# Three segment-max passes of a graph network: the folded buffer is cut from a batch of nine gathers into nine buffers of three, and the fold takes its state from SBUF instead of PSUM

## The chip, the cores and the metric

The kernel runs on one core of a Trainium2 chip. The metric is the device time of one execution in microseconds, the median of three runs. Lower is better.

## The reference, cut to what matters

There are 6250 nodes with 256 float32 features and 100,000 edges, sorted by destination `dst`. The first layer of the network takes the maximum over each node's incoming edges three times, each time of new features. The second layer is an attention over the same edges.

```python
def _pool_max(h, edge_src, edge_dst):
    pooled = segment_max(h[edge_src], edge_dst, num_segments=N)
    cnt = segment_sum(ones, edge_dst, num_segments=N)
    return where((cnt > 0)[:, None], pooled, 0)

h1 = relu(embeddings @ Wp1.T + bp1)
p1 = _pool_max(h1, edge_src, edge_dst)
x  = relu(concatenate([embeddings, p1], 1) @ Wm1.T + bm1)
p2 = _pool_max(x, edge_src, edge_dst)
y2 = relu(concatenate([x, p2], 1) @ Wm2.T + bm2)
x  = _layernorm(y2 + x, ln2_g, ln2_b)
p3 = _pool_max(x, edge_src, edge_dst)
y3 = relu(concatenate([x, p3], 1) @ Wm3.T + bm3)
x  = _layernorm(y3 + x, ln3_g, ln3_b)
```

## The kernel before, in words

**Layout of a max pass.** The 100,000 edges lie as 783 columns (CH) of 128 edges, one in each of the 128 partitions. A partition holds three chains of 261 consecutive edges (C = 3). Within a chain the running maximum goes from one edge to the next, and is reset where a new destination begins: `new = max(old + reset, gathered)`, where reset is 0 or -1e30. That is one VectorE instruction, the fold (L559, 128 rows of 256 features). A step folds one edge of each chain, three folds that don't depend on each other; each depends on the fold of its chain in the step before. Nine columns (J), which are three steps (STEPS), make a batch, and a pass has 87 batches (NB). Three buffers G[b] (UB) hold a batch of nine gathered rows each.

**What each engine does for a batch.** GpSimd waits for the batch's list of indices (`c_eix`) and for the buffer's last store (`s_hs[b]`), and issues nine indirect gathers of 128 rows of 1 KB from the table in DRAM (L533). VectorE waits once for all nine (`s_eg[b]`), and folds in place. The old state is read from PSUM (`state`, `state2`), where ScalarE has copied it: after folds 0 and 1 of a step one copy of two rows (L597), after fold 2 one of the third row (L599), each after a wait on `c_fold`, each announced on `c_state`, which the next step's folds wait for. After the sixth fold VectorE writes the index list of the batch after the next one (`place`, L540). SyncE waits for the last fold and stores the nine folded rows to a history in DRAM, 1152 KB in one DMA (L581).

**What runs beside it.** The helper `staged` writes the order of each engine's instructions out by hand: a list of stages per batch, one after the other, and each engine works it off in that order with no overtaking. Between VectorE's folds stand other pieces ("fillers"). In all passes they include the layer's own tile: TensorE transposes a tile of 128 nodes (L668), ScalarE evacuates it (L651), TensorE multiplies it with a weight (L674), and VectorE adds the bias and keeps the product (`keep`, L637, which waits for the product); 49 tiles, one in each of the first 50 or so batches. In pass 1 come the one-hots that count edges per node (L952, then TensorE at L1120) and part of a sort; in pass 2 the sort (L810, L825); in pass 3 the spread of its result and a bias (L640). After each pass the history's rows are gathered and combined with U to the next features. After the third pass comes the attention layer (L1453, L1869 and on; L2153 and L2163 are its last tiles).

The functions that the change touches are `max_pass` (L518 to L620), the semaphores (L200 and on) and the one-hots' `vector` (L942 to L965).

## Time and profile before

| quantity | value |
|---|---|
| median of 3 runs | 5532.19 us (5524.11 to 5537.15) |
| span of the profiled execution | 5536.0 us, 24899 instructions |
| GpSimd busy | 3489.2 us (63%) |
| VectorE busy | 3357.0 us (61%) |
| ScalarE busy | 1170.9 us (21%) |
| TensorE matmuls busy | 1120.6 us (20%) |
| pass 1, first to last gather | 82.06 to 1249.65 us |
| pass 2 | 1364.13 to 2461.30 us |
| pass 3 | 2588.30 to 3683.20 us |
| gathers of the passes | 2349 of 951 ns on average |
| DMA queues | software 628.59 MB, 38.1% of the engines' span; hardware 409.34 MB, 19.9% |

An engine's busy share is over the whole span; the three passes, their combine stages and the attention have different limits. Instruction groups are named by line, engine and operation; "out<-in" are the tensors written and read. Some PSUM banks have names like tail, wide and trio, and a row carries the name of the bank or neighbouring allocation, so `tail` and `wide` in the fold's rows stand for `state` and `state2`. "Idle before" is the time in which an engine did nothing ahead of an instruction, by what ended it: "issue" is nothing that the profile shows, "remote" a semaphore whose poster it can't name.

### The profile page before, as it was taken

How to read it: one execution, taken by the hardware profiler on the slowest of the kernel's cores; microseconds unless marked ns; L12 is line 12 of the kernel's file. 1: busy time of each engine (PE TensorE's matmuls, PEld its weight loads, DVE VectorE, ACT ScalarE, POOL GpSimd, SP SyncE). 2: the span in 40 equal slices, each digit the busy share in tenths (PEclk: the TensorE clock that was granted, in tenths of full speed). 3: DMA queues.
4: the chain of work that ended last, by engine and by line, in shares of the span. 5: the costliest groups of instructions: out<-in, count | busy, mean ns of one | idle time of the engine just before them, and what ended most of it. 6: DMA issues, size and time to landing. Idle time of an engine off the chain costs nothing. (4 is left out here: it accounts for less than half of the span.)

```text
span 5536.0 us, 24899 instructions
## 1 busy us (share of the span) xinstructions
PE 1120.6 (20%) x4017; PEld 728.3 (13%) x4017; DVE 3357.0 (61%) x6781; ACT 1170.9 (21%) x2663; POOL 3489.2 (63%) x3686
## 2 busy tenths in 40 slices
PE   5333321105222221006222200019400000000005
PEld 4222211004111110005111100016200000000003
DVE  7676666554434434336355433338479888898896
ACT  4222222222222222224222222225100000000001
POOL 4566666665666666665676666654466666666653
PEclk7555555557555555557555555559755555555557
DMA  5555555554555655556555655554477677776763
GB/s 178 170 170 172 173 169 187 183 188 136 197 184 192 203 183 195 185 189 187 199 190 197 217 179 188 188 171 153 139 224 215 212 216 216 224 220 208 218 186 109
DMA packets 325739, 1039.51 MB, mean 188 GB/s; under 512 B 71351, under 2 KB 124740, under 8 KB 292172
## 3 DMA queue, kind: packets, MB, share of 16 engines
q0 software_dynamic: 209408, 628.59, 38.1%
q1 hardware_dynamic: 116172, 409.34, 19.9%
q14 instruction: 125, 1.02, 0.1%
q8 instruction: 34, 0.56, 0.0%
HBM read 649.96 MB, written 388.11 MB: 188 GB/s over the span
## 5 line engine op out<-in xcount | busy, mean ns | idle before, releaser
L533 POOL DMA_INDIRECT G<-tab,ix x2349 | 2233.6, 951 | 1135.8 <-issue 699.7
L559 DVE SCALAR_TENSOR_TENSOR G<-tail,pass_lists,G 128x256 f32<-128x256 f32 x1566 | 696.4, 477 | 1217.8 <-DMA G<-tab,ix 526.8
L1869 POOL DMA_INDIRECT kv<-kvtab,dst_ix x936 | 889.1, 950 | 428.1 <-issue 283.1
L597 ACT ACTIVATE tail<-G 128x512 f32<-128x512 f32 x783 | 470.6, 601 | 1600.4 <-issue 607.7
L599 ACT ACTIVATE wide<-G 128x256 f32<-128x256 f32 x783 | 300.1, 383 | 949.8 <-DVE G L559 521.4
L674 PE MATMUL tail<-weights,hT 128*128 128x256 f32 x588 | 305.0, 674 | 766.3 <-issue 499.6
L559 DVE SCALAR_TENSOR_TENSOR G<-wide,pass_lists,G 128x256 f32<-128x256 f32 x783 | 372.6, 476 | 111.7 <-issue 84.4
L2058 PE MATMUL trio<-ident,state 128*128 128x128 f32 x6 | 2.0, 430 | 1476.8 <-DVEq L2080 1476.8
L674 PEld LDWEIGHTS tail<-weights,hT 128*128 128x128 f32 x588 | 172.7, 324 | 848.9 <-issue 529.1
L1918 DVE TENSOR_TENSOR kv<-kv,wide 128x3072 f32<-128x3072 f32 x78 | 260.8, 3343 | 29.0 <-DMA kv<-kvtab,dst_ix 28.9
L1934 DVE TENSOR_REDUCE s<-kv 128x96 f32<-128x3072 f32 x78 | 260.8, 3343 | 0.0
L2008 ACT ACTIVATE wide<-weights 128x120 f32<-128x120 f32 x78 | 21.4, 274 | 1090.8 <-remote 388.2
L668 PE MATMUL tail<-ident,h 128*128 128x128 f32 x294 | 95.0, 425 | 710.1 <-issue 296.9
L2058 PEld LDWEIGHTS trio<-ident,state 128*128 128x128 f32 x6 | 1.2, 220 | 1477.7 <-DVEq L2080 1477.7
L1120 PE MATMUL trio<-hot 128*128 128x196 bf16 x783 | 140.9, 367 | 240.6 <-DVE hot L952 149.7
L637 DVE TENSOR_TENSOR U<-tail,weights 128x256 f32<-128x256 f32 x147 | 61.3, 417 | 205.8 <-remote 169.5
L952 DVE TENSOR_TENSOR hot<-wide,key_high 128x2156 bf16<-128x2156 f32 x72 | 170.3, 2366 | 10.3 <-issue 5.8
L1394 PE MATMUL trio<-ident,G 128*128 128x128 f32 x18 | 4.5, 424 | 766.0 <-PEq L522 766.0
L668 PEld LDWEIGHTS tail<-ident,h 128*128 128x128 f32 x294 | 41.7, 199 | 818.6 <-issue 760.2
L1120 PEld LDWEIGHTS trio<-hot 128*128 128x128 bf16 x783 | 113.1, 147 | 263.2 <-DVE hot L952 156.5
L1927 DVE TENSOR_TENSOR trio<-kv,wide 128x1536 f32<-128x1536 f32 x78 | 136.5, 1750 | 0.0
L1960 DVE TENSOR_TENSOR pass_lists<-trio,kv 128x1536 f32<-128x1536 f32 x78 | 136.1, 1745 | 0.0
(361 smaller groups left out, 3602.7 us busy)
## 6 DMA issues: line engine op xcount, KB each, us to landing
hist<-G SPq DMA_DIRECT2D x261, 1152.0 KB
G<-tab,ix POOLq DMA_INDIRECT x2349
ahist<-state SPq DMA_DIRECT2D x78, 408.0 KB
tab<-o SPq DMA_DIRECT2D x147, 128.0 KB
kv<-kvtab,dst_ix POOLq DMA_INDIRECT x936
h<-tab SPq DMA_DIRECT2D x98, 128.0 KB
G<-tab SPq DMA_DIRECT2D x98, 128.0 KB
kvtab<-U SPq DMA_DIRECT2D x49, 256.0 KB
```

Of the source, the lines that this page charges most:

```text
L533: g.indirect_dma_start(G[b][:, k, :], None, tab, bass.IndirectOffsetOnAxis(ix[:, b, k:k + 1], 0)).then_inc(s_eg[b].sem, 16)
L559: ins = v.scalar_tensor_tensor(out=G[b][:, k, :], in0=state2 if c == 2 else state[:, c, :], scalar=reset[:, at:at + 1], in1=G[b][:, k, :], ...
L597: a.activation(state, of[:, 0:2, :], ACT.Copy).then_inc(c_state.sem, 1)
L599: a.activation(state2, of[:, 2, :], ACT.Copy).then_inc(c_state.sem, 1)
L668: t = pe.transpose(self.turned[:, k * P:(k + 1) * P], self.h[:, b, k * P:(k + 1) * P], ident[:, :])
L674: m = pe.matmul(self.product, self.hT[:, k * P:(k + 1) * P], self.w[:, k, :], start=(k == 0), stop=(k == KC - 1))
L952: v.tensor_tensor(to[n % self.RING][:, 0:some, :, :].rearrange("p k l e -> p (k l) e"), self.iota[:, None, 0:width].to_broadcast([P, 2 * s ...
L1120: m = pe.matmul(self.sums, self.low[n % self.RING][:, k, :, :], self.high[n % self.RING][:, k, :, :], start=(n == 0 and k == 0), stop=(n = ...
L1869: g.indirect_dma_start(kvs[n % KB][:, k, :], None, kvtab, bass.IndirectOffsetOnAxis(dst_ix[:, at:at + 1], 0)).then_inc(s_kv[n % KB], 16)
L1918: v.tensor_tensor(keys, keys, query[:, None, :, :].to_broadcast([P, SLOT, R, D]), ALU.mult).then_inc(c_scored, 1)
L1927: keep("weighed", i * UB + b, v.tensor_tensor(to.rearrange("p k (d h) -> p k d h", h=HEADS), vals[:, part, :].rearrange("p k (d h) -> p k ...
L1934: keep("sums", i * UB + b, v.tensor_reduce(scores().rearrange("p e r h -> p (e r) h"), kvs[(i * UB + b) % KB][:, :, 0:D].rearrange("p k (h ...
```

## The change

Each of the nine thirds of the three buffers becomes a buffer of its own, with its own semaphores (`s_in[r]` for arrival, `s_kept[r]` for the store). GpSimd waits before every third gather, for the store of that buffer three batches ago, and not once in a batch. VectorE waits for three gathers at a step's first fold, and not for nine at a batch's first. Each fold reads the old state straight from the step before in SBUF, and waits on `c_fold` for the fold three before it, which is its own engine's; all nine folds of a batch post on `c_fold`, where six did. ScalarE's copies, `c_state`, and the waits on it go, those of the one-hots too. SyncE stores each step by itself: three DMAs of 384 KB in place of one of 1152 KB. The sizes, the number of gathers and the order of the fillers on VectorE stay, and so does the place of the index list.

```diff
--- before.py
+++ after.py
@@ -200,10 +200,12 @@
         s_st = [Count(sem(f"s_st{u}")) for u in range(UN)]
         s_put = [sem(f"s_put{u}") for u in range(UN)]
         s_tile = [Count(sem(f"s_tile{b}")) for b in range(UB)]
-        s_eg = [Count(sem(f"s_eg{b}")) for b in range(UB)]
+        RING = UB * STEPS
+        s_in = [Count(sem(f"s_in{r}")) for r in range(RING)]
+        s_kept = [Count(sem(f"s_kept{r}")) for r in range(RING)]
         s_hs = [Count(sem(f"s_hs{b}")) for b in range(UB)]
         c_eix, c_taken, c_batch, c_w, c_e = (Count(sem(n)) for n in ("c_eix", "c_taken", "c_batch", "c_w", "c_e"))
-        c_fold, c_state = Count(sem("c_fold")), Count(sem("c_state"))
+        c_fold = Count(sem("c_fold"))
         s_held = {"vector": sem("s_held_v"), "pool": sem("s_held_p")}
         s_pe = Count(sem("s_pe"))
         s_dve = Count(sem("s_dve"))
@@ -516,8 +518,9 @@
 
 
         def max_pass(G, side, tiles, marks=None, ahead=None):
-            state = bank[3][:, 0:2 * D].rearrange("p (c f) -> p c f", c=2)
-            state2 = bank[6][:, D:2 * D]
+            def rows_of(step):
+                n, j = divmod(step, STEPS)
+                return G[n % UB][:, j * C:(j + 1) * C, :]
 
             with block() as blk:
                 @blk.gpsimd
@@ -528,9 +531,11 @@
 
                     def gather(i, b):
                         g.wait_ge(c_eix.sem, c_eix.of(i, b, UB))
-                        g.wait_ge(s_hs[b].sem, s_hs[b].base + i * 16)
                         for k in range(J):
-                            g.indirect_dma_start(G[b][:, k, :], None, tab, bass.IndirectOffsetOnAxis(ix[:, b, k:k + 1], 0)).then_inc(s_eg[b].sem, 16)
+                            r = b * STEPS + k // C
+                            if k % C == 0 and i:
+                                g.wait_ge(s_kept[r].sem, s_kept[r].base + i * 16)
+                            g.indirect_dma_start(G[b][:, k, :], None, tab, bass.IndirectOffsetOnAxis(ix[:, b, k:k + 1], 0)).then_inc(s_in[r].sem, 16)
                     staged(g, NB, UB, [(0, gather), (0, side.pool(g))])
 
                 @blk.vector
@@ -545,21 +550,19 @@
                     if marks:
                         marks.vector(v)
                     side.start(v)
-                    v.memset(G[UB - 1][:, J - C:J, :], 0.0).then_inc(c_fold.sem, 2)
+                    v.memset(rows_of(UB * STEPS - 1), 0.0).then_inc(c_fold.sem, C)
 
                     def fold(k):
                         def stage(i, b):
                             n, (j, c) = i * UB + b, divmod(k, C)
                             step = n * STEPS + j
-                            if k == 0:
-                                v.wait_ge(s_eg[b].sem, s_eg[b].base + (i * (16 * J) + 16 * J))
-                            if c != 1:
-                                v.wait_ge(c_state.sem, c_state.base + 2 * step + (2 if c else 1))
+                            if c == 0:
+                                arrived = s_in[b * STEPS + j]
+                                v.wait_ge(arrived.sem, arrived.base + (i + 1) * (16 * C))
+                            v.wait_ge(c_fold.sem, c_fold.base + C * step + c + 1)
                             at = c * (CH // C) + step
-                            ins = v.scalar_tensor_tensor(out=G[b][:, k, :], in0=state2 if c == 2 else state[:, c, :], scalar=reset[:, at:at + 1],
-                                                         in1=G[b][:, k, :], op0=ALU.add, op1=ALU.max)
-                            if c:
-                                ins.then_inc(c_fold.sem, 1)
+                            v.scalar_tensor_tensor(out=G[b][:, k, :], in0=rows_of(step - 1 if step else UB * STEPS - 1)[:, c, :], scalar=reset[:, at:at + 1],
+                                                   in1=G[b][:, k, :], op0=ALU.add, op1=ALU.max).then_inc(c_fold.sem, 1)
                             if k == 2 * C - 1:
                                 place((b + 2) % UB, n + 2)
                         return stage
@@ -577,12 +580,14 @@
                     side.sync(sp)
 
                     def store(i, b):
-                        sp.wait_ge(c_fold.sem, c_fold.base + 2 + 2 * STEPS * (i * UB + b + 1))
-                        sp.dma_start(hist_p[:, bass.ds((i * UB + b) * J, J), :], G[b][:, :, :]).then_inc(s_hs[b].sem, 16)
+                        for j in range(STEPS):
+                            step = (i * UB + b) * STEPS + j
+                            sp.wait_ge(c_fold.sem, c_fold.base + C * (step + 2))
+                            sp.dma_start(hist_p[:, step * C:(step + 1) * C, :], G[b][:, j * C:(j + 1) * C, :]).then_inc(s_kept[b * STEPS + j].sem, 16)
                     staged(sp, NB, UB, tiles.sync(sp) + [(0, store)] + (ahead.sync(sp) if ahead else []))
                     side.last_sync(sp)
-                    for b in range(UB):
-                        sp.wait_ge(s_hs[b].sem, s_hs[b].base + (NB // UB) * 16)
+                    for kept in s_kept:
+                        sp.wait_ge(kept.sem, kept.base + (NB // UB) * 16)
 
                 @blk.tensor
                 def _(pe):
@@ -590,31 +595,13 @@
 
                 @blk.scalar
                 def _(a):
-                    def keep_state(step):
-                        n, j = divmod(step, STEPS)
-                        of = G[n % UB][:, j * C:(j + 1) * C, :]
-                        a.wait_ge(c_fold.sem, c_fold.base + 2 * step + 3)
-                        a.activation(state, of[:, 0:2, :], ACT.Copy).then_inc(c_state.sem, 1)
-                        a.wait_ge(c_fold.sem, c_fold.base + 2 * step + 4)
-                        a.activation(state2, of[:, 2, :], ACT.Copy).then_inc(c_state.sem, 1)
-
-                    def keep_step(j):
-                        def stage(i, b):
-                            step = (i * UB + b) * STEPS + j
-                            if step < NB * STEPS - 1:
-                                keep_state(step)
-                        return stage
-
                     fill, evac = tiles.scalar(a)
-                    keep_state(-1)
-                    staged(a, NB, UB, [(0, keep_step(0))] + side.scalar(a, evac) + fill + [(0, keep_step(j)) for j in range(1, STEPS)]
-                           + (ahead.scalar(a) if ahead else []))
+                    staged(a, NB, UB, side.scalar(a, evac) + fill + (ahead.scalar(a) if ahead else []))
             c_eix.close(NB)
-            c_fold.close(2 * NB * STEPS + 2)
-            c_state.close(2 * NB * STEPS)
-            for b in range(UB):
-                s_eg[b].close(NB // UB * 16 * J)
-                s_hs[b].close(NB // UB * 16)
+            c_fold.close(C * (NB * STEPS + 1))
+            for r in range(RING):
+                s_in[r].close(NB // UB * 16 * C)
+                s_kept[r].close(NB // UB * 16)
             if marks:
                 marks.close()
             side.close()
@@ -940,13 +927,12 @@
                     chain.link(v.tensor_copy(self.key_high[:, :, n], self.ti[:, :]))
 
             def vector(self, v):
-                def make(to, key, width, j):
+                def make(to, key, width):
                     def stage(i, b):
                         n = i * UB + b
                         if n >= self.BATCHES:
                             return
                         some = min(self.PER, CH - n * self.PER)
-                        v.wait_ge(c_state.sem, c_state.base + 2 * (n * STEPS + j) + 2)
                         if n >= self.RING:
                             v.wait_ge(self.mm, n - self.RING + 1)
                         v.tensor_tensor(to[n % self.RING][:, 0:some, :, :].rearrange("p k l e -> p (k l) e"), self.iota[:, None, 0:width].to_broadcast([P, 2 * some, width]),
@@ -956,8 +942,8 @@
 
                 def perm(i, b):
                     self.sort.make_perm(v, i * UB + b - 20)
-                fillers = {0: [(0, perm)], 4: [(0, make(self.high, self.key_high, self.HIGH, 1))]} | self.sort.fillers(v, False)
-                fillers[1] = [(0, make(self.low, self.key_low, self.LOW, 0))] + fillers[1]
+                fillers = {0: [(0, perm)], 4: [(0, make(self.high, self.key_high, self.HIGH))]} | self.sort.fillers(v, False)
+                fillers[1] = [(0, make(self.low, self.key_low, self.LOW))] + fillers[1]
                 found = self.find(v)
 
                 def find(i, b):
```

## Rows read from the trace of the kernel before

**Rows 1.** Stages: us, busy (instructions) of each engine, PEclk, DMA share, GB/s.
```profile
82.06:1249.65 1167.59, 279.61 (x1109) 191.71 (x1109) 761.19 (x1567) 289.75 (x614) 744.50 (x783) 0.51 0.52 174
1364.13:2461.30 1097.17, 208.94 (x394) 101.19 (x392) 450.39 (x1134) 261.68 (x566) 742.09 (x783) 0.53 0.57 191
2588.30:3683.20 1094.90, 134.19 (x294) 71.76 (x294) 437.95 (x1034) 266.58 (x570) 749.74 (x787) 0.50 0.58 194
```

**Rows 2.** The gathers' line in pass 1: min/median/max ns, then waits and counts.
```profile
L533 POOL DMA_INDIRECT G<-tab,ix x783: 942/949/1432, 82.1 to 1248.7; - x196
...
  DVE ix L540: 152.1, 21
```

**Rows 3.** Timeline, one gather: start, us, instruction, idle before.
```profile
230.25 0.95 POOL L533 DMA_INDIRECT G<-tab,ix  x1 [0.30 <-issue]
```

**Rows 4.** Groups by line: passes 1 (two rows), 2 (two) and 3 (two).
```profile
L559 DVE SCALAR_TENSOR_TENSOR G<-tail,pass_lists,G 128x256 f32<-128x256 f32 x522 | 235.7, 476 | 146.3 <-DMA G<-tab,ix 95.5 <-issue 32.4 <-ACT tail L597 11.9
...
L637 DVE TENSOR_TENSOR U<-tail,weights 128x256 f32<-128x256 f32 x49 | 20.5, 419 | 190.9 <-remote 168.3 <-issue 22.5
...
L559 DVE SCALAR_TENSOR_TENSOR G<-tail,pass_lists,G 128x256 f32<-128x256 f32 x522 | 232.7, 478 | 484.7 <-DMA G<-tab,ix 253.9 <-issue 151.6 <-ACT tail L597 78.5
...
L825 DVE SCALAR_TENSOR_TENSOR full<-full,both,trio 128x1024 f32<-128x1024 f32 x20 | 25.5, 1277 | 101.3 <-remote 61.0 <-issue 24.4 <-PE trio L856 15.8
...
L559 DVE SCALAR_TENSOR_TENSOR G<-tail,pass_lists,G 128x256 f32<-128x256 f32 x522 | 228.1, 478 | 586.8 <-issue 284.1 <-DMA G<-tab,ix 177.4 <-ACT tail L597 125.0
...
L597 ACT ACTIVATE tail<-G 128x512 f32<-128x512 f32 x261 | 156.9, 601 | 681.7 <-remote 337.1 <-issue 241.3 <-DVE G L559 90.1
```

**Rows 5.** Timeline of pass 3, one step; SPq is SyncE's DMA queue.
```profile
3404.21 0.16 DVE L540 COPY ix<-pass_lists 128x9 int32<-128x9 int32 x1
...
3406.82 0.88 DVE L559 SCALAR_TENSOR_TENSOR G<-tail,pass_lists,G 128x256 f32<-128x256 f32 x2 [2.45 <-issue]
...
3408.52 0.95 POOL L533 DMA_INDIRECT G<-tab,ix  x1 [2.32 <-remote]
...
3410.39 0.60 ACT L597 ACTIVATE tail<-G 128x512 f32<-128x512 f32 x1 [3.10 <-remote]
...
3411.09 0.88 DVE L559 SCALAR_TENSOR_TENSOR G<-tail,pass_lists,G 128x256 f32<-128x256 f32 x2 [3.00 <-ACT tail L597]
3411.09 0.32 SPq L581 DMA_DIRECT2D hist<-G  x1
```

**Rows 6.** Timeline of pass 1, a tile's product and its keep.
```profile
193.73 2.08 PE L674 MATMUL tail<-weights,hT 128*128 128x256 f32 x4 [1.60 <-issue]
...
211.67 0.43 DVE L637 TENSOR_TENSOR U<-tail,weights 128x256 f32<-128x256 f32 x1 [13.38 <-remote]
```

**Rows 7.** Timeline of pass 1, the same batch's first fold and the list.
```profile
233.30 0.88 DVE L559 SCALAR_TENSOR_TENSOR G<-tail,pass_lists,G 128x256 f32<-128x256 f32 x2 [2.10 <-DMA G<-tab,ix]
...
240.17 0.16 DVE L540 COPY ix<-pass_lists 128x9 int32<-128x9 int32 x1
```

**Rows 8.** Groups of VectorE in pass 3, the same operation of other shape.
```profile
L1287 DVE SCALAR_TENSOR_TENSOR trio<-full,b 128x936 f32<-128x936 f32 x1 | 1.1, 1124 | 0.0
L1277 DVE SCALAR_TENSOR_TENSOR full<-full,a 128x936 f32<-128x936 f32 x1 | 1.1, 1122 | 0.0
```

**Rows 9.** Timeline of pass 3 and of the last stage, GpSimd beside VectorE.
```profile
2797.91 0.42 DVE L640 TENSOR_TENSOR X<-X,weights 128x256 f32<-128x256 f32 x1
2797.99 1.15 POOL L533 DMA_INDIRECT G<-tab,ix  x1 [0.31 <-issue]
...
5475.24 0.41 DVE L2153 TENSOR_TENSOR h<-pool,rz 128x256 f32<-128x256 f32 x1
5475.37 1.10 POOL L1453 DMA_INDIRECT pool<-ahist,node_ix  x1 [0.30 <-PE trio L2180]
5475.57 0.41 DVE L2163 TENSOR_TENSOR o<-o,X 128x256 f32<-128x256 f32 x1
```

**Rows 10.** DMA engines' busy tenths, 3411 to 3416 us in 40 slices.
```profile
DMA  0008946969989999989998996599409766999959
```

## The prediction

> **What bounds the kernel now.** On the page GpSimd and VectorE are the busiest engines, and the profile's closing chain lies in the last stage, which the change doesn't touch; so I read the three max passes each by itself. The stage table [rows 1] gives them 1167.6, 1097.2 and 1094.9 us from first to last gather: 3359.7 of the 5536.0 us span. In each GpSimd is busy for about 745 us, VectorE for 761, 450 and 438, so VectorE isn't full in any. Next the gathers' own line [rows 2]: 783 in a pass, median 949 ns, and 0.30 us of issue before each in an even run [rows 3], so one every 1.25 us. That is 783 x 1.25 = 979 us a pass, 11.3 us for a batch of nine. The passes stand 189, 118 and 116 us above that floor, 423 in all. This is what a looser coupling could give back.
>
> Where do they go? The lines by pass [rows 4] differ. In pass 1 VectorE waits little for gathers (95.5 us) but 190.9 us for the product of the layer's tile at L637. In pass 2 the first fold of each pair waits 484.7 us (253.9 for gathers), and the sort's L825 101.3 us. In pass 3 the fold waits 586.8 us, and ScalarE's first copy 681.7 us, 337.1 of it for a release that the trace can't name.
>
> The timeline says what that is. In pass 3 [rows 5] two folds begin at 3406.82 and end at 3407.70, the copy that waits for them starts at 3410.39: 2.7 us later. The list of indices is written at 3404.21 and GpSimd, idle, starts on it at 3408.52, 4.2 us later. So increments of VectorE are seen late here. The copy takes 0.60 us, and the next folds start 0.70 us after it began: one step is 0.88 + 2.7 + 0.7 = 4.3 us, three are 12.8, and the 87 batches of the pass take 12.6 each (1094.9 / 87), over GpSimd's 11.3. Chain, lateness and copy are the bound. In pass 1 it is TensorE's increment: four matmuls end at 195.81, L637 starts at 211.67 [rows 6].
>
> **The change, part by part.**
>
> *Folds begin a step at a time, and the index list goes out earlier.* Of pass 1 [rows 3, 7]: the ninth gather begins at 230.25, the batch's first fold starts at 233.30 (3.05 us on), the list for the batch after next is written at 240.17, and GpSimd would need it at 242.8 (231.5 plus 11.3). Slack 2.6 us; a later wait of VectorE stops GpSimd, which is the 152.1 us of [rows 2]. After: the list needs the sixth gather, not the ninth, 3 x 1.25 = 3.75 us earlier, and folds 0 to 2 with their fillers (half of the 6.9 us from 233.30 to 240.17) already lie beside gathers. Slack 2.6 + 3.75 + about 3 = 9 us, if VectorE is not behind.
>
> *ScalarE's 1566 copies and their semaphore go.* 601 ns for two rows [rows 4], less for the third, all on ScalarE, which is no bound. On the chain of a step they cost 0.70 us plus one crossing. The evacuations on ScalarE no longer stand behind them, which can only bring TensorE's product forward; I count nothing for it, since [rows 6] shows the lateness behind the product. The one-hots' waits for these copies (L949) go as well; they ask for a copy that the folds around them need anyway, so 0.
>
> *Folds read SBUF twice and wait for their own engine.* Duration: an all-SBUF form of the same instruction took 1122 ns for 936 columns, one that writes PSUM 1124 [rows 8]; no change, bounds -2 and +2 ns a fold (476 to 478 by pass), 5 us in all. Each fold now waits for the fold three before it. With no lateness that is hidden behind two folds of 0.40 us (0.88 less 0.48). With the 2.7 us of [rows 5] a step is 0.48 + 2.7 = 3.2 us against 4.3 before, three are 9.5, under GpSimd's 11.3. The point from which VectorE would bound is (11.3 / 3) - 0.48 = 3.3 us of lateness. Behind a fold that waits stand the index list, the sort's steps and L637, for which GpSimd, TensorE and SP wait in turn.
>
> *GpSimd and the second SBUF input.* Of the adds that read SBUF twice [rows 9]: one of 0.42 us starts at 2797.91, the gather at 2797.99 takes 1.15 us and not 0.95. The add has 0.34 us left at that start, and the excess is 0.20, 0.14 less. A fold of 0.48 us can so hit in 0.34 of the 1.25 us between two gathers, by 0.17 on average: 0.05 us a gather, 38 us in a pass that GpSimd bounds. Bounds: 0 (the phase always misses) and 0.9 us a step if a gather had to sit out all three folds. I take 0.05, because at 5475.37 a gather came in at the end of the first of two such operations (0.15 longer), though the second began at 5475.57 within it.
> The Trainium skill, SBUF — State Buffer (Who interferes with whom), says that "A DVE instruction with two SBUF inputs contends with a GpSimd instruction that reads SBUF". By that rule every one of the 2349 folds becomes a contender where none is now, and the 1.15 us agrees that an indirect gather counts as a reader. The same section also infers that `tensor_tensor` doesn't disturb descriptor generation; by that the term would be 0 and the sum 76 us lower. The trace sides with the first.
>
> *Nine buffers, three stores a batch.* 261 stores of 1152 KB become 783 of 384. One filled the DMA engines from 3411.4 to the end of the stretch, 3416 [rows 10], some 4.6 us; a third of it some 2. SP issues each in 0.32 us [rows 5], 1 us a batch of 11.3. A buffer of a step is needed again after nine steps, 33.8 us, and is done after 3.05 to the fold + 1.4 of folds + 3 of lateness + 2 of store = 9.5; its wait goes, and nothing takes its place. 0, bounds -30 and +40 for the more frequent DMAs beside gathers.
>
> **Sum.** Pass 1: GpSimd's 152.1 us of waits for the list are 21 of 7.2 us. The slack grows by 6.4, but has to be won back between two of them (VectorE is busy for 761.19 / 87 = 8.7 of a batch's 11.3 us, so by 2.6 a batch) while L637's 190.9 us stay: I take half, 76 off, and put the port's term into the rest: 1092. Pass 2: 979 + 38 + 28, the last for those of L825's 20 waits (101.3 us) that outlast 9 us, an estimate, = 1045. Pass 3: 979 + 38 + 23, a quarter us a batch for steps over 3.3 us late, = 1040. Together 3177, that is 183 less. At the end of each pass one step is folded and stored and not nine rows: 5 us each, 15. Gain 198. The profiled span of 5536.0 lies 4 us over the median 5532.2 and inside the runs' 5524 to 5537, so I go by the median: 5532 - 198 = 5334, say 5335 us. The cases of this forecast run from 5240 to 5440.
>
> **Rivals.**
> *A, the lateness goes with the crossings.* Then L637's stalls shrink and all passes run at GpSimd's pace plus 38: 3 x 1017 = 3051, gain 309 + 15: 5210. For: in pass 1 gathers go at 1.25 us and folds of a batch take 6.9 us [rows 7] with none late. Against: TensorE's increment was late where no copy was concerned [rows 6].
> *B, nothing is gained.* Pass 1 keeps its 1168 (L637 decides), and passes 2 and 3 change one wait for another: 5525.
> *C, slower: late increments grow with their number.* VectorE's folds post 9 a batch and not 6, and each fold now waits for one. If lateness goes with their number, 2.7 us become 2.7 x 1.5 = 4.1, a step 4.5 and a batch 13.6 against 12.8. It decides from 3.3 us. At that pace three passes are 3 x 87 x 13.6 = 3550, 190 more, less the 15 at the ends: 5710. Against: SP and ScalarE no longer take two increments of every step each, and in [rows 7] none is late.
> *D, slower: the port.* A gather sits out the whole train of three folds: 0.6 us a step on average, 783 steps, 470 us on GpSimd's path: 3 x 979 + 470, and pass 1's 76, are 3483, 123 more, less the 15: 5640. Against: 5475.37 of [rows 9].
>
> **How the numbers follow.** Forecast 0.50, A 0.20, B 0.08, C 0.13, D 0.09. Faster by over 0.2% (11 us; less can't be told from no change here) is the forecast and A, with some of B: 0.71. Same: 0.07. Slower: C and D: 0.22. Range 5170 to 5590: below lies the part of A that reaches the floor (5532 - 438 = 5094), above most of C and D.
>
> **What would show it.** L533's waits for the index list gone in pass 1 or nearly, no wait for `hist`. L533's mean about 1.00 us, with many at 1.0 to 1.3, in a fold's phase; D shows 1.5 and more. L559 at 476 ns still. Passes at 1092, 1045 and 1040. L637 still stalled for 150 us; if not, A. In C, L559 waits for L559, with batches over 13 us in pass 3. Stores in flight for 2 us, and SP never behind. I am wrong if pass 3 isn't the one that gains its share while pass 1 is: then the chain was not its bound.

## The result, and the profile after

The changed kernel takes 5553.7 us (19 runs, 5535.5 to 5562.3) against 5532.2 us before: a ratio of 1.0039, 95% interval 1.0030 to 1.0048, 21 us slower. The forecast was 5335 us. At other times the chip was met in another condition, in which the kernel before takes 4921 to 4926 us and no increment of a semaphore is seen late (an increment is an engine's signal that an instruction is done; it is late when its record, and what waits for it, come well after the instruction's end). I call the two the late and the prompt condition. Each ratio compares kernels in one condition, and the two kernels were compared in both: in the prompt one it is 4969.2 against 4921.4, 1.0100 (1.0083 to 1.0117). So the change is slower in either, for two reasons that have to be kept apart.

The stage table of the changed kernel in the late condition, from first to last gather of each pass (columns as in [rows 1]):

```profile
81.90:1289.10 1207.20, 262.50 (x1107) 192.67 (x1107) 765.15 (x1573) 41.30 (x95) 768.24 (x783) 0.54 0.53 170
1395.00:2498.80 1103.80, 205.89 (x394) 99.84 (x392) 462.98 (x1140) 18.83 (x49) 760.16 (x783) 0.53 0.60 191
2616.10:3713.30 1097.20, 133.97 (x294) 71.61 (x294) 456.58 (x1036) 22.14 (x55) 769.78 (x785) 0.50 0.60 193
```

Against [rows 1] the passes are 39.6, 6.6 and 2.3 us longer, 48.5 together. The profiled span grew by 24.6 (5560.6 less 5536.0), since the stretches between and after the passes are 24 us shorter (15 were forecast). ScalarE went from 290, 262 and 267 us busy to 41, 19 and 22: the copies are gone, and the kernel is no faster for it. GpSimd is 24, 18 and 20 us busier with the same 783 gathers, from [rows 1]'s 744.50, 742.09 and 749.74. The groups of the page by line:

```profile
L538 POOL DMA_INDIRECT G<-tab,ix x2349 | 2296.2, 978 | 1122.6 <-issue 693.5
L564 DVE SCALAR_TENSOR_TENSOR G<-G,pass_lists 128x256 f32<-128x256 f32 x2349 | 1060.5, 480 | 1262.5 <-DMA G<-tab,ix 470.0
L624 DVE TENSOR_TENSOR U<-tail,weights 128x256 f32<-128x256 f32 x147 | 61.2, 417 | 263.0 <-remote 261.8
```

A gather is 978 ns on average, where it was 951; a fold is 480 ns, where it was 476 or 477. The keep of the tile's product (L637 before, L624 now) waits 263.0 us where it waited 205.8. The gathers' line in pass 1, for [rows 2]:

```profile
L538 POOL DMA_INDIRECT G<-tab,ix x783: 940/947/1787, 81.9 to 1288.1; - x196
...
  issue: 232.4, 763
  DVE ix L545: 206.4, 19
```

GpSimd's waits for the index list, which the change was to take away, went from 152.1 us to 206.4, in fewer and longer pieces: 19 of 10.9 us and not 21 of 7.2. One of them, in the timeline of the changed kernel (start, us, instruction, idle before):

```profile
250.47 2.08 PE L661 MATMUL tail<-weights,hT 128*128 128x256 f32 x4 [1.60 <-issue]
...
269.98 0.95 POOL L538 DMA_INDIRECT G<-tab,ix  x1 [0.30 <-issue]
...
275.96 0.42 DVE L624 TENSOR_TENSOR U<-tail,weights 128x256 f32<-128x256 f32 x1 [20.89 <-remote]
276.53 0.66 PE L655 MATMUL tail<-ident,h 128*128 128x128 f32 x2 [23.99 <-DVE U L624]
...
284.11 0.16 DVE L545 COPY ix<-pass_lists 128x9 int32<-128x9 int32 x1
...
284.54 0.94 POOL L538 DMA_INDIRECT G<-tab,ix  x1 [13.62 <-DVE ix L545]
```

The product is done at 252.55, and the trace records its increment at 275.94. VectorE, which has been idle since 255.07, goes on at 275.96: 23.4 us after the product and 5.04 us after GpSimd's last gather has ended (270.92). It then works off the batch in hand, and needs 8.2 us to the next list. GpSimd stands for 13.6 us. In pass 1 the keep stalls thirteen times for 13 to 23 us, and eleven of the stalls end 4.2 to 5.3 us after GpSimd's last gather. That looks like no fixed lateness, but like a stall that ends when GpSimd has run dry. In the kernel before the keep's stalls were of 5 to 16 us (13.38 in [rows 6]), and only the six longest ended 2.9 to 4.9 us after a last gather, the others while GpSimd went on.

### The profile page after: what moved, and what is told of

It reads as the page before. It is cut to its first block and busy times, and to the rows that moved or that the text cites. A ratio compares the mean times of both kernels' runs of the same rounds, so it can differ in the third digit from the quotient of the medians.

```text
span 5560.6 us, 24243 instructions
## 1 busy us (share of the span) xinstructions
PE 1102.2 (20%) x4017; PEld 729.8 (13%) x4017; DVE 3387.0 (61%) x6781; ACT 428.0 (8%) x1097; POOL 3551.0 (64%) x3686
## 5 line engine op out<-in xcount | busy, mean ns | idle before, releaser
L538 POOL DMA_INDIRECT G<-tab,ix x2349 | 2296.2, 978 | 1122.6 <-issue 693.5
L564 DVE SCALAR_TENSOR_TENSOR G<-G,pass_lists 128x256 f32<-128x256 f32 x2349 | 1060.5, 480 | 1262.5 <-DMA G<-tab,ix 470.0
L624 DVE TENSOR_TENSOR U<-tail,weights 128x256 f32<-128x256 f32 x147 | 61.2, 417 | 263.0 <-remote 261.8
L638 ACT ACTIVATE hT<-tail 128x256 f32<-128x256 f32 x147 | 56.5, 384 | 1934.8 <-PE tail L655 945.8
L843 PE MATMUL trio<-full,perm 128*128 128x512 f32 x112 | 88.6, 938 | 239.5 <-issue 170.3
L1913 DVE TENSOR_TENSOR kv<-kv,wide 128x1536 f32<-128x1536 f32 x78 | 135.9, 1743 | 0.0
L1439 POOL DMA_INDIRECT pool<-hist,node_ix x98 | 96.4, 983 | 51.1 <-PE trio L1571 25.0
```

Of the source, the lines that this page charges most:

```text
L538: g.indirect_dma_start(G[b][:, k, :], None, tab, bass.IndirectOffsetOnAxis(ix[:, b, k:k + 1], 0)).then_inc(s_in[r].sem, 16)
L564: v.scalar_tensor_tensor(out=G[b][:, k, :], in0=rows_of(step - 1 if step else UB * STEPS - 1)[:, c, :], scalar=reset[:, at:at + 1], in1=G[ ...
L1439: g.indirect_dma_start(pool[:, u, 0:width], None, table, bass.IndirectOffsetOnAxis(rows_of[:, t:t + 1], 0)).then_inc(s_gat[u].sem, 16)
L1913: keep("weighed", i * UB + b, v.tensor_tensor(to.rearrange("p k (d h) -> p k d h", h=HEADS), vals[:, part, :].rearrange("p k (d h) -> p k ...
```

## Experiments

Four groups. The first two were run in the late condition, the last two in the prompt one. "List" is the index list that `place` writes. Times are medians, each with its ratio to the kernel before as measured beside it.

### What ends the stalls (late condition)

**The list after the ninth fold and not the sixth**, in the changed kernel:

```diff
-                            if k == 2 * C - 1:
+                            if k == J - 1:
                                 place((b + 2) % UB, n + 2)
```

> The changed kernel, with the index list for the batch after next written after the ninth fold and not after the sixth. The trace of the changed kernel has in pass 1 thirteen stalls of VectorE at L624 (the keep of the tile's product) of 13 to 22 us, and twelve of them end about 5 us (4.2 to 5.3) after GpSimd's last gather has ended. Theory S (starved increment): TensorE's increment isn't seen as long as gathers follow each other, and the stall ends when GpSimd has run out of lists. Then a later list, which leaves GpSimd a batch less in hand when VectorE stalls at fold 7, makes the stall some 11 us shorter (about 9 to 11 us in place of 20), and GpSimd's gap is 5 us plus the one fold up to the list, 6 to 7 us and not 13: pass 1 goes from 1207 us to about 1120, whole kernel 5480. Rival F (fixed lateness: the increment takes some 20 us whatever GpSimd does): the stalls stay at 20 us, GpSimd is dry for longer (16 us and more for each), pass 1 at about 1250 us, whole kernel 5600 or more.

(Counted again it is eleven stalls and not twelve.) 5478.7 us, 0.9887 (0.9855 to 0.9919), and pass 1 1126.5 us. Moving the list later, that is giving slack away, made the kernel some 75 us faster than the changed one. One stall of it:

```profile
230.03 1.85 PE L661 MATMUL tail<-weights,hT 128*128 128x256 f32 x4
...
243.51 0.95 POOL L538 DMA_INDIRECT G<-tab,ix  x1 [0.30 <-issue]
...
248.29 0.42 DVE L624 TENSOR_TENSOR U<-tail,weights 128x256 f32<-128x256 f32 x1 [11.04 <-remote]
...
249.02 0.17 DVE L545 COPY ix<-pass_lists 128x9 int32<-128x9 int32 x1
...
249.46 0.94 POOL L538 DMA_INDIRECT G<-tab,ix  x1 [5.00 <-DVE ix L545]
```

GpSimd has no list beyond the batch in hand and stops at 244.46; the keep goes on 3.8 us later; the list stands right behind it, and GpSimd's gap is 5.0 us and not 13.6. The twelve longest stalls of the keep are 9.4 to 11.1 us long, and five more 5.3 to 7.4. Theory S, starvation, stands here; a fixed 20 us falls.

**A rest of GpSimd of 1.2 us a batch**, in the changed kernel:

```diff
+                    g.memset(pause[:, :], 0.0).then_inc(c_rest.sem, 1)
+                    def rest(i, b):
+                        for m in range(3):
+                            g.wait_ge(c_rest.sem, c_rest.base + (i * UB + b) * 3 + m + 1)
+                            g.memset(pause[:, :], 0.0).then_inc(c_rest.sem, 1)
-                    staged(g, NB, UB, [(0, gather), (0, side.pool(g))])
+                    staged(g, NB, UB, [(0, gather), (0, rest), (0, side.pool(g))])
```

> The changed kernel with a rest of GpSimd of about 1 us after the nine gathers of each batch (three small memsets, each waiting for the one before). Theory S, if a short gap is enough to let increments through: the stalls at L624 of 13 us and more are gone or down to a few, GpSimd no longer waits 206 us for the list in pass 1, and pass 1 is 87 batches of 11.3 + 0.3 + 1.2 us, about 1110 us; passes 2 and 3 stay near 1100. Whole kernel about 5460. If an increment needs GpSimd to be dry for 5 us, or in rival F, the stalls stay as they are: pass 1 1207 plus the rests that no stall hides, 1270 us, whole kernel 5600 to 5750.

5500.7 us, 0.9937 (0.9908 to 0.9965). The gathers' line in pass 1 and the stage table:

```profile
L538 POOL DMA_INDIRECT G<-tab,ix x783: 942/946/1828, 80.7 to 1196.2; - x196
...
  issue: 242.2, 782
  DVE ix L551: 0.4, 1
```

```profile
80.70:1197.20 1116.50, 259.16 (x1107) 193.15 (x1107) 772.01 (x1573) 41.26 (x95) 864.15 (x1042) 0.56 0.57 184
1303.40:2412.70 1109.30, 211.84 (x394) 102.26 (x392) 460.97 (x1140) 18.77 (x49) 856.96 (x1041) 0.53 0.59 190
2531.60:3652.90 1121.30, 133.94 (x294) 71.64 (x294) 445.82 (x1041) 22.08 (x55) 868.33 (x1044) 0.50 0.59 190
```

Every stall of the keep is gone, and 0.4 us of waits for the list are left of 206.4. Of the increments that the trace records none of VectorE's comes late, and in pass 1 eleven of TensorE's, by 1.1 to 4.9 us. But passes 2 and 3 did not get faster: 12.75 and 12.89 us a batch (1109.3 and 1121.3 over 87).

**One memset of 0.4 us a batch** in its place, in the changed kernel and in one with nine buffers and the state in PSUM:

```diff
-                        for m in range(3):
-                            g.wait_ge(c_rest.sem, c_rest.base + (i * UB + b) * 3 + m + 1)
-                            g.memset(pause[:, :], 0.0).then_inc(c_rest.sem, 1)
+                        g.wait_ge(c_rest.sem, c_rest.base + (i * UB + b) + 1)
+                        g.memset(pause[:, :], 0.0).then_inc(c_rest.sem, 1)
```

> The changed kernel with one memset of 128x300 a batch on GpSimd (about 0.4 us) in place of three. With three, which took 1.17 us, every batch took 12.7 us and not one increment of TensorE or VectorE was seen late. Theory G (any gap lets increments through): batches take 11.3 + 0.3 + 0.5 = 12.1 us, no stalls of 10 us at L624, passes at about 1050 to 1060 us, whole kernel 5330 to 5370. Theory R (GpSimd's rate: gathers at 1.25 us fill something that takes only about one in 1.4 us, and increments stand behind what is in it until it drains): the lateness comes back with the shorter rest, though later and less often, and the batches' mean stays at 12.5 to 12.9 us whatever the rest is, as it is in pass 2 and 3 of every kernel so far (12.57 to 12.77); whole kernel 5480 to 5540.

> Nine buffers with the state copied to PSUM by ScalarE as in the kernel before, and one memset of 128x300 a batch on GpSimd. Theory G: 12.0 us a batch, about 0.25 us less than with the SBUF state, since no gather is lengthened: passes at 1040 us, whole kernel 5300 to 5340. Theory R: the batches' mean stays at 12.5 to 12.8 us, and since here no gather is lengthened by a fold, more of the lateness stays than with the SBUF state: 5480 to 5520.

5571.1 us, 1.0085 (1.0055 to 1.0116), and 5539.5 us, 1.0028 (1.0012 to 1.0043). The stage table of the first:

```profile
80.90:1287.80 1206.90, 262.26 (x1107) 192.58 (x1107) 767.04 (x1573) 41.31 (x95) 798.55 (x870) 0.54 0.53 170
1394.80:2501.00 1106.20, 206.60 (x394) 99.52 (x392) 464.03 (x1133) 18.82 (x49) 793.60 (x870) 0.54 0.59 190
```

The stalls of 16 to 22 us are back, and pass 2 takes 12.7 us a batch again. So not any gap will do. Theory R had the batches right and the whole kernels too low (5480 to 5540 and 5480 to 5520), since pass 1 kept its stalls. What R says, that in this condition gathers go at 1.25 us for a while only and lateness makes up the rest until the mean is 12.6 us for nine, fits the means; no run shows what would set such a rate. By the stage tables, passes 2 and 3 took 12.61 and 12.59 us a batch before, 12.69 and 12.61 after, 12.56 and 12.63 with the late list, 12.71 and 12.63 with the short rest. The batches behind these means differ: the median one of pass 3 took 11.5 us before and 12.15 with the short rest.

**The three memsets in the kernel before:**

> The kernel before with the three memsets (1.2 us) a batch on GpSimd. If its late increments are of the same kind as those of the changed kernel, they vanish here too: pass 1 without stalls at the keep, all batches near 12.5 us, pass 1 at 1090 to 1100 us (from 1168), passes 2 and 3 at 1090 to 1100 as they were; whole kernel 5455 to 5475. If the lateness of before came from ScalarE's copies and their waits: the stalls stay and the rests come on top, 5550 to 5650.

5526.6 us, 1.0007 (0.9986 to 1.0029): neither. A miss on pass 1:

```profile
82.30:1254.10 1171.80, 281.18 (x1109) 192.76 (x1109) 761.60 (x1567) 289.89 (x616) 834.98 (x1042) 0.50 0.52 175
1366.70:2459.50 1092.80, 208.60 (x394) 100.75 (x392) 448.20 (x1134) 260.61 (x567) 832.14 (x1042) 0.54 0.57 193
```

Its batches run at 12.48 us where the changed kernel's ran at 12.8 (its gathers aren't lengthened), and pass 1 keeps seven keep stalls of 14 to 16 us, most of them 85 us apart, where the changed kernel's stand 59 apart. That 12.48 is a little too fast and 12.8 slow enough, with the rate that lasts between them, would fit, but it is only argued: the two kernels differ in more than their pace.

### Which part of the change does what (late condition)

**Nine buffers alone** (arrival, release and store by step; the state copied to PSUM as before), and **SBUF state alone** (three buffers of nine gathers, one store a batch, no copies). The first is the change without its fold, the second the change with, in place of its waits and stores:

```diff
# nine buffers alone: the fold stays that of before
+                            if c == 0:
+                                arrived = s_in[b * STEPS + j]
+                                v.wait_ge(arrived.sem, arrived.base + (i + 1) * (16 * C))
                             if c != 1:
                                 v.wait_ge(c_state.sem, c_state.base + 2 * step + (2 if c else 1))
# SBUF state alone: the batch's waits and store stay those of before
                             if k == 0:
                                 v.wait_ge(s_eg[b].sem, s_eg[b].base + (i * (16 * J) + 16 * J))
+                            v.wait_ge(c_fold.sem, c_fold.base + C * step + c + 1)
```

> The kernel before with the nine buffers alone: arrival, release and store by steps of three gathers, and the state still copied to PSUM by ScalarE. Theory P (the port): the 65 to 70 us by which gathers got longer in the changed kernel (2296 us busy in place of 2234, 400 gathers over 1.0 us in place of 20) come from the folds' second SBUF input; here the gathers are back at 949 ns and under 30 are over 1.0 us. With theory S the stalls at the keep stay as long as in the changed kernel (some 15 to 20 us), since the list goes out as early. Whole kernel 5553 less 65, plus what the copies cost on the chain: 5490 to 5530. Rival N (more and smaller stores make gathers longer): the gathers are as long as in the changed kernel, about 978 ns, and the kernel is at 5550 to 5580.

> The changed kernel with the three buffers of nine gathers back: arrival of all nine, one store a batch, one release a batch; the state is still read from SBUF and ScalarE has no copies. Theory P: gathers as long as in the changed kernel (mean about 978 ns, some 400 over 1.0 us), so 60 to 70 us over the kernel before. Theory S: the stalls at the keep are about as long as in the kernel before (5 to 15 us), since the list goes out as late as there. Whole kernel 5532 + 65, less the 0.7 us a step that the copies took where the chain bound (up to 60 us): 5540 to 5600. Rival N: gathers at 950 ns, whole kernel 5480 to 5530.

5510.0 us, 0.9954 (0.9937 to 0.9972), and 5553.8 us, 1.0038 (1.0016 to 1.0060). The gathers' groups of the first and of the second:

```profile
L537 POOL DMA_INDIRECT G<-tab,ix x2349 | 2234.8, 951 | 1116.8 <-issue 706.0 <-remote 236.6 <-DVE ix L544 170.2
```

```profile
L535 POOL DMA_INDIRECT G<-tab,ix x2349 | 2290.6, 975 | 1123.9 <-issue 680.6 <-DVE ix L542 231.5 <-remote 163.3
```

The longer gathers belong to the SBUF state alone (975 ns against 951); three times the stores don't lengthen one. Pass 1 is 1138.6 us with nine buffers and 1216.3 with the SBUF state, against 1167.6: the whole loss of pass 1 comes with the SBUF state and the missing copies. With theory S I expected stalls as long as the changed kernel's in the first and as short as before's in the second; it is the other way round, 7 to 12.6 us in the first, all but one ending while GpSimd goes on, and 15.5 to 17.5 us in the second but for one, all these ending 4.8 to 5.3 us after GpSimd has run dry. So how early the list goes out isn't by itself what made the stalls long. The halves' times, -19 and +25 us, don't add up to the whole's +21 here either; how they act on each other isn't shown.

**One increment a step in place of three:**

```diff
-                            v.wait_ge(c_fold.sem, c_fold.base + C * step + c + 1)
+                            if c == 0:
+                                v.wait_ge(c_fold.sem, c_fold.base + step + 1)
...
+                            if c == C - 1:
+                                ins.then_inc(c_fold.sem, 1)
```

> The changed kernel with one increment of c_fold a step (by the third fold) and not three, so 3 a batch and not 9; a step's first fold waits for the whole step before. Theory Q (lateness grows with the number of increments that VectorE posts): with 6 of some 20 a batch gone, the stalls at L624 are rarer or shorter, GpSimd's waits of over 0.6 us in pass 1 fall from 206 us by a third or more, whole kernel 5450 to 5500. If the number of increments is of no weight: stalls as in the changed kernel, time within 10 us of it (5545 to 5565), or some us more where no filler stands between two steps.

5570.0 us, 1.0087 (1.0056 to 1.0117), GpSimd's waits of over 0.6 us in pass 1 217 us and not 206. Rival C of the forecast had lateness grow with the number of VectorE's increments. With two thirds of the folds' increments gone the kernel isn't faster and GpSimd waits no less, so C isn't the cause of the loss. But the stalls are others: the longest of the keep is 16.7 us and not 22.6, its waits in pass 1 are 210.9 us and not 260.5, and eleven of the nineteen stalls of over 4 us end while GpSimd goes on. So the number of increments, or the waits on them, has some weight that these runs don't separate.

### The two kernels in the prompt condition

**ScalarE's copies back, of a constant and read by nobody; one of three rows stored in pass 3; the list late in the kernel before; both remedies of pass 1 together.** The edits of the first two, in the changed kernel:

```diff
# idle copies, before and after those of the tile as in the kernel before
+                                a.wait_ge(c_fold.sem, c_fold.base + C * (step + 1) + 2)
+                                a.wait_ge(c_copy.sem, c_copy.base + 2 * step + 1)
+                                a.activation(bank[3][:, 0:2 * D], reset[:, 0:2 * D], ACT.Copy).then_inc(c_copy.sem, 1)
+                                a.wait_ge(c_fold.sem, c_fold.base + C * (step + 2))
+                                a.wait_ge(c_copy.sem, c_copy.base + 2 * step + 2)
+                                a.activation(bank[3][:, 0:D], reset[:, 0:D], ACT.Copy).then_inc(c_copy.sem, 1)
# a third of the stores in pass 3
+                        kept_rows = 1 if ahead else C
-                            sp.dma_start(hist_p[:, step * C:(step + 1) * C, :], G[b][:, j * C:(j + 1) * C, :])
+                            sp.dma_start(hist_p[:, step * C:step * C + kept_rows, :], G[b][:, j * C:j * C + kept_rows, :])
```

> The changed kernel with ScalarE's 1560 copies back, but of a constant and read by nobody: they wait for the folds as those of before did, and no fold waits for them. Pass 1 was 1207 us with the folds on SBUF, and 1139 us with nine buffers and the state in PSUM. If ScalarE's activity and its waits are what shortens TensorE's stalls: pass 1 near 1140 to 1160, whole kernel 5490 to 5515. If it is the form of the fold or its wait for its own engine (or that VectorE runs ahead without the crossing): pass 1 at 1195 to 1220, whole kernel 5540 to 5570.

> The changed kernel, but in pass 3 only one of a step's three rows is stored, 128 KB and not 384 KB; the history's other rows stay those of pass 2, so the output is another. Theory R has 12.6 us a batch as a sustained rate; what sets it is open. If the stores' bytes take part in it (they share the DMA engines with the gathers): pass 3's batches fall to 11.4 to 12.0 us, few increments late, pass 3 at 1000 to 1045 us, whole kernel 5460 to 5510. If GpSimd's own path sets it, whatever the DMA engines move: pass 3 stays at 1090 to 1100 us, 12.6 us a batch, with the same lateness, whole kernel within 10 us of 5553.

> The kernel before with the index list written after the ninth fold. Theory S (a starved increment is let through when GpSimd runs dry, so a lead of GpSimd only lengthens the stall): the worst stalls of pass 1 are shorter and GpSimd's gap behind each is 5 us and not 12, pass 1 at 1100 to 1130 us in place of 1168; passes 2 and 3 stay at 12.5 to 12.7 us a batch (theory R: that is GpSimd's sustained rate). Whole kernel 5460 to 5495. If slack is what counts in pass 1, as my forecast had it: a list later by three folds (3.4 us) makes GpSimd's waits longer, pass 1 at 1220 us, whole kernel 5580.

> The changed kernel with both remedies in pass 1 (three memsets a batch on GpSimd and the list after the ninth fold) and the later list alone in passes 2 and 3. Theory R: pass 1 runs at 12.7 to 12.8 us a batch without late increments, as it did with the rests alone: 1110 to 1117 us; passes 2 and 3 at 1093 to 1100. Together 3305 to 3315, whole kernel 5460 to 5470, the fastest so far by a little. If the later list costs slack once the increments are prompt, pass 1 is over 1130.

These four met the prompt condition, so none tested what it was written for. In this order they took 4974.2 us (1.0110, 1.0092 to 1.0129), 4974.0 (1.0113, 1.0095 to 1.0132), 5009.2 (1.0180, 1.0158 to 1.0202) and 5074.9 (1.0313, 1.0295 to 1.0332). What they do say: both remedies are costs here. The rests took pass 1 of the changed kernel to 1117.2 us, against 1013.1 without them (below). The late list alone, in its passes 2 and 3, cost 2.6 and 2.1 us; in the kernel before it cost 62, 21 and 4 us in the three passes. Their stage tables, the changed kernel with both remedies and then the kernel before with the late list:

```profile
79.90:1197.10 1117.20, 261.35 (x1107) 194.19 (x1107) 773.94 (x1573) 41.27 (x95) 864.88 (x1041) 0.55 0.57 184
1291.40:2285.20 993.80, 211.71 (x394) 101.75 (x392) 459.08 (x1140) 18.77 (x49) 755.57 (x783) 0.54 0.66 212
2399.10:3406.80 1007.70, 134.00 (x294) 71.70 (x294) 436.08 (x1041) 22.09 (x55) 768.85 (x785) 0.50 0.66 212
```

```profile
81.40:1126.30 1044.90, 279.51 (x1109) 192.48 (x1109) 759.78 (x1567) 289.86 (x616) 741.88 (x783) 0.50 0.58 196
1225.60:2224.80 999.20, 208.11 (x394) 100.53 (x392) 450.10 (x1134) 260.23 (x567) 740.75 (x783) 0.54 0.62 211
2342.60:3334.80 992.20, 134.04 (x294) 71.74 (x294) 427.96 (x1035) 256.98 (x573) 750.96 (x785) 0.50 0.64 214
```

So the looser coupling does give slack, and the changed kernel can lose three folds of it almost for nothing; there is only nothing else for it to cover. The second and the third were tried again, with the two kernels themselves.

> The kernel before, unchanged, for its trace beside the next three. In the last call the kernel before took 4921.6 us and not 5532, and no kernel of that call showed a late increment. If this call is like that one: GpSimd starts a gather every 1.25 us, passes at 1000 to 1020, 985 and 985 us, gathers of 949 ns, 4920 us. If it is like the earlier ones: 5525 to 5540 us, batches of 12.6 us on average in passes 2 and 3.

> The changed kernel, unchanged. If the call is like the last one (no late increments): passes at about 1010, 993 and 1010 us, each 15 to 30 us over the kernel before by gathers of 975 to 985 ns in place of 949 (the port), all of it on GpSimd's path: 4965 to 4980 us, 1% slower than before. If it is like the earlier ones: 5545 to 5565 us, 0.4% slower, with twelve or so stalls of 13 to 22 us in pass 1.

4921.3 us (1.0001, 0.9990 to 1.0011) and 4969.2 us (1.0100, 1.0083 to 1.0117). The stage tables, the kernel before and then the changed one:

```profile
80.40:1063.40 983.00, 281.58 (x1109) 192.93 (x1109) 760.87 (x1567) 289.87 (x616) 741.79 (x783) 0.51 0.61 208
1162.60:2141.20 978.60, 208.29 (x394) 100.97 (x392) 445.39 (x1134) 260.22 (x567) 740.34 (x783) 0.54 0.63 215
2258.80:3246.70 987.90, 134.02 (x294) 71.69 (x294) 430.98 (x1035) 256.98 (x573) 749.01 (x785) 0.50 0.64 215
```

```profile
79.20:1092.30 1013.10, 257.36 (x1107) 193.21 (x1107) 773.02 (x1573) 41.30 (x95) 774.85 (x783) 0.56 0.62 202
1187.00:2178.20 991.20, 211.55 (x394) 101.76 (x392) 456.21 (x1140) 18.82 (x49) 752.88 (x783) 0.54 0.66 213
2291.70:3297.30 1005.60, 133.97 (x294) 71.65 (x294) 436.25 (x1041) 22.14 (x55) 766.75 (x785) 0.50 0.66 212
```

The kernel before stands within 9 us of the forecast's floor of 979 us in all three passes (1000 to 1020 us were expected in the first): when no increment is late, its three buffers and its copies cost next to nothing inside the passes, and there is next to nothing for a looser coupling to win there. The changed kernel's passes are 30.1, 12.6 and 17.7 us longer, and GpSimd is 33.1, 12.5 and 17.7 us busier. Its extra time in the passes is the gathers' extra time. In its trace the 776 gathers that start while a fold runs take 1030 ns on average and the other 1573 949 ns; in the kernel before, whose folds read PSUM, the two are 946 and 950 ns. One such gather in the changed kernel's timeline, and one behind it without a fold at its start:

```profile
700.97 0.48 DVE L564 SCALAR_TENSOR_TENSOR G<-G,pass_lists 128x256 f32<-128x256 f32 x1
...
701.18 1.12 POOL L538 DMA_INDIRECT G<-tab,ix  x1 [0.30 <-issue]
702.60 0.95 POOL L538 DMA_INDIRECT G<-tab,ix  x1 [0.30 <-issue]
```

> The kernel before with the index list after the ninth fold, again. Where increments are late: theory S has pass 1 at 1100 to 1130 us in place of 1168, with GpSimd's gaps at 5 us each, and the whole kernel at 5460 to 5495; slack as my forecast had it would give 1220 us and 5580. Where none is late: 5009 us as in the last call, 1.8% slower than before, since only slack counts there.

> The changed kernel with one of three rows stored in pass 3, again. Where increments are late: pass 3's batches at 11.4 to 12.0 us if the stores' bytes take part in the sustained rate of 12.6 us, or at 12.6 us with the same lateness if they don't. Where none is late: as the changed kernel within 5 us, 4974 us.

5007.1 us (1.0175, 1.0158 to 1.0192) and 4973.4 us (1.0103, 1.0086 to 1.0120), both as expected for the prompt condition. The first is the price of slack in the kernel before when it is the only thing that counts: a list three folds later costs 86 us.

### The two halves in the prompt condition

> Nine buffers with the state in PSUM, again, for the conditions in which no increment is late. There the changed kernel is 48 us slower than the one before (4969 against 4921). Theory P (the port: the folds' second SBUF input lengthens gathers, and that is the whole loss): here gathers are back at 949 ns, the passes lose nothing and gain at their ends, 4900 to 4920 us, at or a little under the kernel before. Rival N (the more frequent stores or waits cost): 4930 to 4970. If increments are late again: 5500 to 5520, as in the first call.

> Three buffers of nine gathers with the state in SBUF and no copies, again, for the conditions in which no increment is late. Theory P: gathers of 970 to 985 ns and 60 to 75 us over the kernel before: 4975 to 5000 us, since the shorter ends of the passes that nine buffers give are missing. Rival N: 4921 within 10 us. If increments are late again: 5545 to 5565, as in the first call.

4908.9 us, 0.9968 (0.9955 to 0.9980), and 4992.3 us, 1.0137 (1.0120 to 1.0154). The gathers' groups, nine buffers and then SBUF state:

```profile
L537 POOL DMA_INDIRECT G<-tab,ix x2349 | 2228.0, 949 | 726.1 <-issue 687.9 <-DVE ix L544 38.2
```

```profile
L535 POOL DMA_INDIRECT G<-tab,ix x2349 | 2299.2, 979 | 727.6 <-issue 674.6 <-DMA hist<-G 37.8 <-DVE ix L542 15.1
```

The halves add up here: -17 and +66 are +49, and the whole change is +48. Nine buffers with the state left in PSUM beat both kernels in both conditions, if by little (0.9954 and 0.9968); it is the version to keep.

## Why the prediction was wrong

- *The floor, "one every 1.25 us ... 979 us a pass".* The step that failed, in the late condition, from whose trace the forecast was made. 1.25 us is the spacing of one gather from the next in an even run [rows 3], and I took it for a rate that lasts. In the late condition what lasts is 12.6 us for nine gathers: passes 2 and 3 came out at 12.5 to 12.75 us a batch in every kernel without long rests, whatever the coupling. That is an observed mean; its cause is open. The mean stood in the table before: 1097.2 and 1094.9 us are the same number for two passes with quite different work beside the gathers [rows 1]. I explained the second by a chain of 12.8 us a batch (0.88 + 2.7 + 0.7, three times), worked out from one late step [rows 5], and the agreement with 12.6 was luck: the median batch of that pass took 11.5 us, and the 32 of 87 that took over 13 us made the mean. The forecast was 1045 and 1040 us for these passes, against 1103.8 and 1097.2. These two passes are 116 us of the miss of 219; pass 1 is another 115, and the ends gave back 9. (The forecast's 23 us for pass 3 is also a slip: a quarter us in 87 batches is 22.)
- *"Chain, lateness and copy are the bound"; the copies' removal.* Wrong in both conditions. With the copies gone pass 3 didn't move (1094.9 to 1097.2), and where nothing is late the kernel with the copies is within 9 us of the floor.
- *"A looser coupling": slack from 2.6 to 9 us in pass 1.* Slack was gained (the late list's prices in the prompt condition say so; its size wasn't measured), and the sign of its worth was wrong. I took the stall as a given length that slack could cover. In the changed kernel eleven of the thirteen long stalls end only when GpSimd has run dry, and there slack covers nothing. GpSimd waited 206.4 us for lists and not the 76 that the forecast left; pass 1 took 1207.2 us and not 1092. The late list, which has less slack, took 81 us off pass 1.
- *Rows 5 and 6 as "late".* The observation was right and carried the wrong weight: I charged one lateness to the chain and left the other as it was ("while L637's 190.9 us stay"). Rival A, that it vanishes, and rival C, that it grows, both took it as a property of VectorE's and TensorE's traffic. The rests in the changed kernel show that GpSimd's pace takes part in it; in the kernel before they left seven long stalls, so they don't show that it is the pace alone.
- *The port.* Right in its mechanism and in its order of size. 0.05 us a gather were forecast and 27 ns measured (976 against 949), about half: 63 us of GpSimd's time over three passes, where the forecast had 38 in each. The late condition hides most of it in passes 2 and 3, where the mean batch stays near 12.6 us in any case; the prompt one shows it whole. The Trainium skill, SBUF — State Buffer (Who interferes with whom), has a VectorE instruction with two SBUF inputs contend with a GpSimd instruction that reads SBUF. The traces agree: 975 and 979 ns with the SBUF state alone against 951 and 949 with nine buffers alone, in the late and the prompt condition. Rival D, that a gather sits out all three folds, falls: that would be 0.6 us a step, and it is three times 27 ns.
- *Durations, stores, ends.* Nearly as forecast: folds of 480 ns on average where 476 to 478 and 2 ns more at most were expected, 7 us in all; three times the stores without effect on the gathers; and the ends shorter by 24 us (late) and 13 (prompt) for 15.
- *Which rival came nearest.* B, "passes 2 and 3 change one wait for another", with 0.08. It describes passes 2 and 3 well (they moved by 6.6 and 2.3 us), and has pass 1 at 1168 us where it took 1207.2.

Open: what sets the rate of 12.6 us (the kernel that stores a third met the prompt condition both times); what makes a condition late or prompt; and why, with the folds on SBUF and no copies, a late increment of TensorE mostly waits for GpSimd to run dry, while with the state in PSUM it often gets through after some 10 us. Idle copies were meant to tell that and met the prompt condition. One rival for the first two is untested: that the recording of the trace takes part. Every trace of the late condition lacks many records of increments (the changed kernel's pass 1 has 847 of VectorE's 1577), every trace of the prompt condition has them all, and no run here is known to be without recording.

## What to carry to other kernels

The shortest spacing of an engine's instructions is a rate only if some stretch keeps it up: divide the stage by its count first, and where two stages of different work give the same quotient, look for one common limit before two chains. A wait that ends a fixed time after another engine falls idle isn't covered by slack that keeps this engine busy; let that engine rest, or keep its lead short, but measure it: where no increment was late both cost time. Reading a second operand from SBUF and not PSUM can cost GpSimd's gathers more than the copy that it saves, when the copy is on an idle engine.

## What the runs showed of the hardware that was not expected

- In the late condition increments of TensorE are seen up to 28 us late and VectorE's up to 9 us while GpSimd issues indirect gathers every 1.25 us: a product of the changed kernel's pass 1 ends at 130.11, its increment is recorded at 158.16. ScalarE's, as far as they are recorded, are all within 0.1 us. With 1.2 us of rest in each batch of nine gathers the changed kernel has no stall of the keep left, with 0.4 us it has them again; in the kernel before 1.2 us leave seven of 14 to 16 us.
- The same kernel takes 5532 or 4921 us at different times: in the one condition nine gathers take 12.6 us on average in passes 2 and 3 and increments come late, in the other 11.2 to 11.4 us and none does. Both were met on one and the same chip, 25 minutes apart.
- The remedies depend on it: the late list is worth some 75 us in the changed kernel in the late condition; in the prompt one it costs 2 to 3 us a pass there, in passes 2 and 3, and 86 us in the kernel before.
- A gather that starts while a fold with two SBUF inputs is running takes 0.08 us longer on average in the prompt condition (1030 against 949 ns), 0.2 us and more in some; averaged over all gathers it is 27 ns. The add at L640 of the kernel before, also of two SBUF inputs, does the same: the 15 gathers that start in it take 1090 ns on average there, and those that start beside no VectorE instruction 946.
